# First slots of each attention placed between the last steps of the stage ahead of it

## The reference

```
x = ln(x + L0_attn(x))   # gated linear recurrence over the tokens, then an MLP
x = ln(x + L0_ffn(x))    # ternary weights, gelu
x = ln(x + L1_attn(x))   # 16 heads of 8: softmax(q k' / sqrt(8) + causal mask) v
x = ln(x + L1_ffn(x))    # top-2 of 8 experts with capacity, plus a shared expert
x = ln(x + L2_attn(x))   # 16 heads, softmax with a position bias (alibi)
x = ln(x + L2_ffn(x))    # see below
x = ln(x + L3_attn(x))   # 16 heads, softmax with one extra "void" key and value
x = ln(x + L3_ffn(x))    # layernorm, top-2 of 8 gated experts
```

```
s = einsum('btd,dm->btm', x, Win) + bin_          # m = 64
h = relu(s[..., None] * W1 + b1)                  # 64 x 16 = 1024 hidden units
g = einsum('btmh,mh->btm', h, W2) + b2
out = einsum('btm,md->btd', g, Wout) + bout
```

## Time and profile before

| | us |
|---|---|
| median of 3 runs | 1348.02 (1346.12 to 1348.26) |
| profiled execution | 1348.4, of which the span from first to last instruction 1347.1 |
| PE busy in the span | 1134.0 (84%) |
| DVE busy | 782.4 (58%) |
| ACT busy | 631.5 (47%) |
| POOL busy | 235.8 (18%) |
| longest chain | PE 71%, DVE 15%, ACT 5% |

### The profile page before, as it was taken

How to read it: one execution, slowest core, us unless ns; L and a number is a source line. 1 busy time by engine, 2 the same in 40 slices (tenths; PEclk the granted TensorE clock), 3 DMA queues, 4 the chain that set the end, 5 groups by cost and what they waited for, 6 DMA issues and landing times.

```text
span 1347.1 us, 18286 instructions
## 1 busy us (share of the span) xinstructions
PE 1134.0 (84%) x6879; PEld 562.7 (42%) x6879; DVE 782.4 (58%) x1472; ACT 631.5 (47%) x1218; POOL 235.8 (18%) x395
## 2 busy tenths in 40 slices
PE   6598669999785994549999989959999965999994
PEld 3266424444553762303333336622222233555552
DVE  5965656776440005487888833388888845333334
ACT  5574335666322441316777755427777741212220
POOL 8336200000154443100000021001111031000001
PEclk9799779999887997659999999969999985999997
DMA  6901722221611102641222100641222020000001
GB/s 165 180 0 52 217 97 83 85 89 38 202 36 53 57 23 72 179 164 56 75 75 72 35 1 25 175 136 64 75 78 76 29 97 1 0 0 1 0 0 32
DMA packets 77902, 97.55 MB, mean 72 GB/s; under 512 B 10099, under 2 KB 58794, under 8 KB 77030
## 3 DMA queue, kind: packets, MB, share of 16 engines
q1 hardware_dynamic: 69734, 90.06, 22.2%
q10 hardware_dynamic: 5680, 3.04, 0.8%
q0 software_dynamic: 2400, 3.29, 0.8%
HBM read 68.12 MB, written 32.55 MB: 75 GB/s over the span
## 4 chain that ended last, share of the span: by engine, by line
PE 71%; DVE 15%; ACT 5%; issue 3%; POOL 3%; DMA 2%; SPq 1%; ACTq 0%; DVEq 0%; POOLq 0%
PE PS L542 15%; PE PS L713 13%; PE PS L727 12%; PE PS L691 8%; PE PS L547 5%; PE PS L948 4%; PE PS L833 3%; DVE negm L1352 3%; PE PS L827 2%; PE PS L716 2%; PE PS L694 2%; PE PS L735 2%; ACT arena L1110 1%; DVE bn L1199 1%; DVE X L1210 1%
## 5 line engine op out<-in xcount | busy, mean ns | idle before, releaser
L1352 DVE TENSOR_REDUCE negm<-PS 128x2 f32<-128x1024 f32 (+3 forms) x384 | 404.7, 1088 | 113.4 <-PE PS L691 58.1
L1046 ACT ACTIVATE arena<-PS 128x512 f32<-128x512 f32 (+3 forms) x768 | 362.9, 548 | 200.5 <-PE PS L716 131.5
L713 PE MATMUL PS<-arena 128*128 128x512 bf16 (+3 forms) x768 | 234.0, 364 | 17.2 <-DMA arena<-mT 9.4
L727 PE MATMUL PS<-arena,VPAD 128*32 128x512 f32 (+3 forms) x1536 | 186.0, 555 | 0.1
L691 PE MATMUL PS<-arena 32*128 32x512 bf16 (+3 forms) x768 | 145.8, 382 | 37.4 <-DVE negm L1352 15.7
L691 PEld LDWEIGHTS PS<-arena 32*128 32x128 bf16 x768 | 36.3, 92 | 229.5 <-issue 100.9
L713 PEld LDWEIGHTS PS<-arena 128*128 128x128 bf16 x768 | 69.6, 98 | 127.4 <-issue 65.4
L542 PE MATMUL PS<-arena,VPAD 128*128 128x512 f32 x256 | 120.8, 609 | 0.9 <-DVE arena L1648 0.8
L542 PE MATMUL PS<-arena,W 128*128 128x512 f32 x200 | 104.8, 658 | 6.0 <-ACT arena L971 4.9
L1858 POOL CAST nmp<-negm 128x16 bf16<-128x16 f32 x48 | 9.5, 198 | 563.9 <-DVE negm L1352 388.4
L1171 ACT ACTIVATE arena<-PS 128x512 f32<-128x512 f32 x64 | 38.2, 597 | 144.9 <-PE PS L542 144.9
(11 more groups left out here) (259 smaller groups left out, 1410.4 us busy)
## 6 DMA issues: line engine op xcount, KB each, us to landing
arena<-score_q SPq DMA_DIRECT2D x48, 288.0 KB
arena<-score_k SPq DMA_DIRECT2D x48, 288.0 KB
arena<-max_parts SPq DMA_DIRECT2D x48, 256.0 KB
max_parts<-arena SPq DMA_DIRECT2D x36, 256.0 KB
arena<-fixed_rows SPq DMA_DIRECT2D x6, 896.0 KB
score_k<-arena SPq DMA_DIRECT2D x36, 128.0 KB
score_q<-arena SPq DMA_DIRECT2D x12, 384.0 KB
slots_x<-zeros SPq DMA_DIRECT2D x1, 2580.0 KB, 22.9
```

The lines of the kernel that those rows point to most:

```text
L713: mm = pe.matmul(PS[:, b, q0:S], OK[s][:, r, kt * P:(kt + 1) * P], OQ[s][:, r, q0:S], start=True, stop=True)
L727: mm = pe.matmul(PS[32 * r:32 * r + 32, 7, q0:S], VP[:, u, kt, r, :], PB[:, kt % 2, r, q0:S], start=(kt == 0), stop=True, skip_group_check ...
L1046: act.activation(PB[:, kt % 2, r, q0:S], PS[:, 4 + use % 3, q0:S], ACT.Exp, scale=slope(u % G, r) if o["slope"] else 1.0).then_inc(exped, 1)
L1352: vec.tensor_reduce(negm[:, u % 2, 2 * rp:2 * rp + 2, qt], PS[:, 2 * (use % 2):2 * (use % 2) + 2, 0:nk], AX.X, ALU.max, negate=True).then_ ...
```

## The change

The maxima run 14 slots ahead of the scores (`LEAD`). `attention(a)` no longer runs a loop: on PE, DVE and POOL it returns a function `slot(t)`, and the strings of turns of the stage ahead have a letter R wherever the next slot is to be done; all 14 slots ahead of slot 0 stand there on PE and DVE, and `rest` does the others. The strings were also given other orders of lanes. ACT's loop is as before. The waits for a lane's values and keys stand at the first use: lanes 0 and 1 at maxima jobs 0 and 1, whose bank pairs are theirs, lanes 2 and 3 at the first scores.

A unit's output is transposed at slot 8u + 12, not 8u + 11. The spills are two functions, each with a semaphore of its own; ahead of slot 0 only lane 0 is spilled, the halves of lanes 1 to 3 at slots 1, 6, 22, 30, 46 and 54. The loads of the maxima operands stand ahead of those of the score operands. `mT` is sent from POOL's queue. The constant rows are only 2 or 11 partitions per buffer; the rest is cleared by POOL with a memset of 128 x 4096 floats for each of two lanes, at slots -14 and -12.

In layer 2 the feed-forward part has one product per lane, of `Win` repeated twice (128 columns), and the eight ReLUs all read that one bank with other scales and biases; hidden units are numbered anew on the host.

```diff
-LEAD = 12
+LEAD = 14
+BLANK_SLOTS = (-LEAD, -LEAD + 2)
+SPILL_SLOTS = {1: (1, 0), 6: (1, 1), 22: (2, 0), 30: (2, 1), 46: (3, 0), 54: (3, 1)}
...
-COMBINE_TENSOR, COMBINE_TENSOR_TURNS = words("tr qk v"), "003112031232"
+COMBINE_TENSOR, COMBINE_TENSOR_TURNS = words("tr qk v"), "001101332RRR32RRRRRRR2RRRR"
...
+def rest(turns):
+    return range(-LEAD + turns.count("R"), JOBS + 5)
...
         def output_unit(t):
-            return (t - 11) // 8 if t >= 11 and (t - 11) % 8 == 0 else None
+            return (t - 12) // 8 if t >= 12 and (t - 12) % 8 == 0 else None
...
             def attention(a):
-                for t in slots():
-                    if turned_unit(t) is not None:
-                        max_rows(a, turned_unit(t))
-                    if t % 8 == 0 and t // 8 + 3 < UNITS:
-                        attention_loads(a, t // 8 + 3)
+                for t in range(JOBS):
+                    if t in SPILL_SLOTS or t % 8 == 0 and t // 8 + 3 < UNITS:
+                        sp.wait_ge(scored, score_use[a, t] + 1)
+                    if t in SPILL_SLOTS:
+                        c, part = SPILL_SLOTS[t]
+                        (max_spills, score_spills)[part](c, f"p{a + 1}", a)
+                    if t % 8 == 0 and t // 8 + 3 < UNITS:
+                        maxima_load(a, t // 8 + 3)
+                        score_load(a, t // 8 + 3)
...
             def spills_and_first_loads(a, tag):
-                spills(0, tag, a)
+                max_spills(0, tag, a)
                 constant_rows(a, 0)
-                attention_loads(a, 0)
-                spills(1, tag, a)
+                maxima_load(a, 0)
+                score_spills(0, tag, a)
+                maxima_load(a, 1)
+                score_load(a, 0)
+                score_load(a, 1)
                 constant_rows(a, 1)
-                attention_loads(a, 1)
-                spills(2, tag, a)
-                spills(3, tag, a)
+                maxima_load(a, 2)
+                score_load(a, 2)
...
                 def maxima(job):
...
+                    if job < 2:
+                        banks_left(job)
...
+                    if job == 0:
+                        banks_left(2)
+                        banks_left(3)
+                    if job in (0, 16):
+                        pe.wait_ge(rows_in[job // 16], 16 * (a + 1))
...
-                    elif step == "f01":
+                    elif step == "c.s":
                         pe.wait_ge(*A.at(c, "ch.xT"))
-                        for n in range(2):
-                            product(c, (L.B, L.A)[n], win[:, n * P:(n + 1) * P], L.xT, f"ch.f{n}")
...
+                        product(c, L.B, win, L.xT, "ch.s")
...
-                        activated(c, f"ch.f{n}", (L.B, L.A)[n % 2], L.h8[:, n, :], ACT.Relu, f"ch.h{n}",
+                        activated(c, "ch.s", L.B, L.h8[:, n, :], ACT.Relu, f"ch.h{n}",
                                   scale=cw1[:, n:n + 1], bias=cb1[:, n:n + 1])
...
-            layer2()
-            attention(2)
+            layer2(attend[2])
+            for t in rest(LAYER2_TENSOR_TURNS):
+                attend[2](t)
...
+                def blank_rows_of(c):
+                    pool.wait_ge(*(T.at(c, "t.sum"), V.at(c, "cb.tot"), T.at(c, "ch.out"))[a])
+                    pool.memset(view(arena, lanes[c].big, [2 * R * S]), 0.0).then_inc(blanked[c], 1)
+
+                def row_of_maxima(u):
+                    s, KR = u % NB, key_rows(a)
+                    if u < NB:
+                        pool.wait_ge(rows_in[u // 2], 16 * (a + 1))
+                    pool.wait_ge(*ring_freed[ring_use[a, "turned", u]])
+                    pool.dma_start(OQ[s][KR:KR + 2].rearrange("a r (t q) -> a (r t) q", t=CT), mT[:, s, :]).then_inc(max_row[s], 16)
```

248 lines of the change are left out of this document (144 added, 104 removed).

## The result

The kernel after takes 1310.07 us, median of four runs (1307.22 to 1312.18), beside 1348.14 before (1346.12 to 1348.39): 0.9719 of it, 95% interval 0.9701 to 0.9738. The profiled execution took 1308.36 us with a span of 1306.8, where the sum of the prediction was 1307.9 and the forecast 1306.

The account below looks back on a forecast made before the run. PE was taken to bound the attentions, with DVE next and the three starts to be shortened. Terms -12.4 - 14.7 - 20 + 7.7 - 1.1 = -40.5 from 1348.4 gave 1307.9, forecast 1306 us; 8-in-10 range 1286 to 1327.

Parts of the forecast that it names:

- First scores at 171.7: Start of first attention: wait for `mT` goes, DVE sets the pace from about 146; first scores a gain of 12.4 us.
- First scores of the second attention, gain 14.7: Start of second attention: memsets delay lane 0's split to 547.5, then DVE always has work; first scores at about 583.5.
- Third attention, gain 20: Layer 2: 24 us of products go, some 20 us of maxima are hidden, ACT and memsets take back the rest.
- ACT without gaps for 27 us: Sign in layer 2: ACT runs its ReLUs without gaps, PE idle until the first lane's eighth ReLU.
- Ring: Two pairs of banks: PE waits behind each output, 13 units in each of attentions two and three, costing 7.7 us.
- At nothing: Edits costed at 0: `mT` from POOL's queue, late spills, new lane orders (-3 to +3), the clock at the starts.
- rival 4: Attention units: `mT` from POOL's queue late in every unit; slower than before from 8.4 us on; chance 0.06 with other mishaps.
- The clock, 0: Three attention starts: PE as sparse as before ahead of slot 0, so again 1.2 GHz; at most half of 10 us returned.
- Rival 1: Starts: memsets don't hold DVE (-3.5 and -4 us), and PE keeps its clock (-9); about 1290 us; chance 0.22.
- Rival 2: Layer 2: clock falls where ACT sets the pace; output products and projections at half speed, 12 to 16 us; 1320; chance 0.15.
- Rival 3: Starts: slots move but DVE and PE only change places, lanes 2 and 3 late by the maxima; about 1325 us; chance 0.12.
- three signs of being wrong: Lane 2's or 3's steps late by maxima; PE's clock 0.50 during output products; PE waiting for `mT` in the units.

Follow-up runs that it names:

- slots last: Kernel after with all 14 slots ahead of slot 0 behind the stage's last step on PE and DVE: 1324.0 us, ratio 0.9755 of the kernel before.
- combine order on before: Kernel before with only the orders of lanes ahead of the second attention as in the kernel after: 1357.5 us, ratio 1.0012 of the kernel before.

## Why the prediction was right, and where it was not

**The sum** was right to 0.2 us, by terms that were off by 4 either way. That closeness is luck: the same kernel run again had 0.9763 of its kernel before, which is 6 us more on this scale.

**First scores at 171.7:** 167.5. The term that was mis-sized is the maxima, 13.4 us for 14. They were taken from a stretch of before that holds waits; without them 13 take 9.2 (0.41, 1.01, 1.52, 0.96, 2.68 and so on, of which the shortest read 128 columns of a bank). The start at 144.2 was forecast for 146. It holds that the wait for `mT` goes and DVE is next.

**First scores of the second attention, gain 14.7:** 14.0. The two effects of the memsets are there as worked out, 2.3 us of delay of the inverse root and 3.0 on a normalisation. But the mechanism was half told. The total of DVE's work was right, and that DVE would have something to do all the time; the forecast did not say that before it had not, for 18.0 us, and that the order of lanes, not the slots, ends this.

**Third attention, gain 20:** 16.7. The step that failed is "some 20 us of maxima go under the tail": with the slots last start 3 is as short. What the runs show in its place: 6 us with the single product, nothing more with the new orders (105.3), and 13 with the new transfers and what goes with them (92.2), which the prediction had at nothing. The ReLUs were costed too high, 26 us for 22 (0.68 each), but they stand in two pieces with 2.96 us of waiting between, as PE reaches lane 3's product only after the first output, and the sign "ACT without gaps for 27 us" did not come. PE's first transposes came at 816.45, which is 843.5 on the scale of before (its attention ended 27.1 us later), as forecast; lane 3's output, normalisation and the first maxima followed 2.3 us later than forecast, partly at 1.2 GHz. That the products would not bring their 24 us at once was right on the kernel before; how much ACT's pace covers in the kernel after is open.

**Ring, +7.7:** 7.6 us of waits for the row maxima (3.0 and 4.6, 13 each, 0.23 and 0.35 us, as worked out), 5.3 us in the lengths of the two attentions with the two slots less.

**At nothing:** this is where the prediction was weakest. `mT` from POOL's queue was costed at nothing against a late landing only; it landed in 4.7 us, so rival 4 did not come about. But with `mT` from SP in its new place the first attention is 15.7 us longer, and without the late spills the three are 14.6. Each of them is needed by the others: they add nothing to the sum since they prevent what the rest would cause. The stage behind the last attention lost 1 to 2 us by its new orders, within the 3 that were given.

**The clock, 0:** right for the scores. The grant was 0.50 for the first 10 us of the second attention's and 7 of the third's, as long as before. Ahead of the third it was low for longer, and the sum has no term for that.

**Rivals.** Rival 1's first half is refuted (4.09 and 7.17 us beside memsets). Rival 2: the grant fell to 0.50 in layer 2 from 780 to 790 us, where PE waits for ReLUs, and was 1.00 in the output products of the first three lanes (790.45 to 812.9), so its price of 12 to 16 us did not come; but it was 0.50 again over the last lanes' projections, from 841.4 to 848.2 and from 851.6 on. What these cost is not separated from DVE's pace there. Rival 3 is right for starts 2 and 3 as a mechanism, which was one of the three signs of being wrong, and wrong in its time, as the orders and the transfers brought what the slots did not. Its own terms give 1328, not 1325; rival 4's come out slower than before from 8.1 us on, not 8.4. By the Trainium skill's rule (SBUF — State Buffer, Who interferes with whom) the weighted sums, with their two SBUF inputs, are not held by a memset, which reads nothing: the rows at 514.89 and 516.07 agree, 1.11 us beside a memset.

## What to carry to other kernels

Before a gain is put down to overlap, add up what the bounding engine waited for in that stretch of before: here 18 us of DVE's were waiting, and an order of lanes ended it. Edits that look free are to be tried for what the others do without them: an earlier start only moved the wait to the transfers, until these had been made lighter and put in another order. A small urgent transfer wants a place ahead of the loads of its queue, or another queue. A memset on POOL has a place where it holds neither a normalisation nor an inverse root, but putting a wait in front of it puts the wait in front of all that is behind it.

## What was not expected of the hardware

An 8 KB transfer took 6.6 to 7.8 us until PE had it from SP's queue behind loads of 832 KB, and 4.7 (median) to its landing from POOL's in another kernel with the same loads just ahead. And ACT's wait of 18 to 33 us in the shared expert, in all eight profiles of two sets and in none of the six others, whatever the kernel. In the eighth profile PE's own products come one to four at a time there, with up to 1.7 us between them in which it waited for nothing that the profile shows (393 to 420 us), and much the same in the combine order on before; what holds the engines stays open.
